# The last batch's routing beside the first half's twenty fixed groups, in one block, in the first expert stage

## The reference

```python
logits = x @ router_w.T + expert_bias[None, :]
probs = sigmoid(logits)
top_w, top_idx = top_k(probs, 8)                   # 8 of 160 experts
top_w = top_w / (sum(top_w) + 1e-09) * 2.5
h1 = silu(einsum('th,eih->eti', x, w_gate))        # 128 -> 64, each expert
routed = einsum('eti,ehi->th', h1 * combine, w_down)
shared = silu(x @ w_gate_shared.T) @ w_down_shared.T
return routed + shared
```

## Time and profile before

| | |
|---|---|
| median of 3 runs | 2836.28 us (2828.25 to 2845.3) |
| profiled execution | 2840.0 us, its span 2838.8 us |
| granted TensorE clock, mean | 0.806 |
| busy: PE / DVE / ACT / POOL | 2002.9 / 1632.1 / 1087.8 / 1264.2 us |
| routing of the last batch | about 862 to 916 us |
| experts, first half / second half | 916 to 1089 us / 1089 to 1275 us |

### The profile page before, as it was taken

One profiled execution on the slowest core, in us unless ns is written; L12 is line 12 of the kernel. 1 busy time (PEld: TensorE's weight loads), 2 busy tenths in 40 slices (PEclk: granted clock), 3 DMA queues, 4 the chain that ended last, 5 costly groups with the idle time before them and its releaser, 6 DMA issues. The chain is left out here.

```text
span 2838.8 us, 45747 instructions
## 1 busy us (share of the span) xinstructions
PE 2002.9 (71%) x15915; PEld 1145.2 (40%) x15915; DVE 1632.1 (57%) x4701; ACT 1087.8 (38%) x2067; POOL 1264.2 (45%) x1244
## 2 busy tenths in 40 slices
PE   5898887877882775665878889888888467676000
PEld 3456455455461554542333333333342255454000
DVE  5457585784777231457776878688783533145222
ACT  0263453453540443440545544443444144444000
POOL 0043166566673444543434420430443444456775
PEclk8899989999995897885787878787887589878555
DMA  9200001000034664554132130121100656555221
GB/s 377 95 1 4 1 6 35 24 12 34 19 131 154 195 209 158 186 177 123 29 90 50 48 82 21 50 74 33 50 29 26 252 182 211 181 187 175 70 59 45
DMA packets 132475, 275.70 MB, mean 97 GB/s; under 512 B 29411, under 2 KB 44387, under 8 KB 127891
## 3 DMA queue, kind: packets, MB, share of 16 engines
q1 hardware_dynamic: 99478, 205.60, 21.8%
q0 software_dynamic: 32768, 67.17, 7.8%
HBM read 146.34 MB, written 125.93 MB: 96 GB/s over the span
## 5 line engine op out<-in xcount | busy, mean ns | idle before, releaser
L1473 POOL DMA_INDIRECT slots_in<-g_xs,g_place x512 | 508.5, 993 | 500.7 <-ACT b_pT L2521 188.6
L2521 ACT ACTIVATE b_pT<-b_psE 128x512 f32<-128x512 f32 (+3 forms) x768 | 330.4, 491 | 469.6 <-PE b_psE L2420 228.9
L2271 DVE TENSOR_REDUCE b_peak<-b_psM 128x1 f32<-128x512 f32 (+3 forms) x768 | 394.5, 551 | 141.5 <-PE b_psM L2403 87.0
L1498 POOL DMA_INDIRECT r_xs<-slots_out,g_place x336 | 333.0, 991 | 312.4 <-ACT b_pT L2521 183.3
L2400 PE MATMUL b_psM<-b_kS,b_qS 72*128 72x512 bf16 (+3 forms) x768 | 283.9, 402 | 66.2 <-DVE b_peak L2271 34.0
L2416 PE MATMUL b_psE<-b_qS,b_kS 75*128 75x512 bf16 (+3 forms) x768 | 258.5, 391 | 57.1 <-ACT b_pT L2521 39.5
L1498 POOL DMA_INDIRECT g_xs<-slots_out,g_place x176 | 172.4, 980 | 124.4 <-issue 48.1
L2060 DVE COPY m_staged_w<-wgd 128x192 f32 x512 | 98.3, 263 | 222.5 <-PE m_psY L2002 114.5
L2060 DVE COPY n_staged_w<-wgd 128x192 f32 x512 | 97.8, 262 | 207.7 <-PE n_psY L2002 147.8
L2430 PE MATMUL b_psV<-b_pT,b_vb 128*32 128x512 f32 (+3 forms) x1536 | 197.3, 597 | 2.5 <-ACT b_pT L2521 2.2
L2400 PEld LDWEIGHTS b_psM<-b_kS,b_qS 72*128 72x128 bf16 x768 | 83.5, 111 | 264.7 <-DVE b_peak L2271 138.6
(11 more groups left out here) (640 smaller groups left out, 4167.3 us busy)
## 6 DMA issues: line engine op xcount, KB each, us to landing
wgd<-in_w_gdT SPq DMA_DIRECT2D x8, 3840.0 KB, 23.0
slots_in<-g_xs SPq DMA_DIRECT2D x26, 1024.0 KB
m_rows<-slots_in SPq DMA_DIRECT2D x104, 256.0 KB
slots_out<-m_y SPq DMA_DIRECT2D x104, 256.0 KB
n_rows<-slots_in SPq DMA_DIRECT2D x104, 256.0 KB
slots_out<-n_y SPq DMA_DIRECT2D x104, 256.0 KB
b_qS<-q_parts SPq DMA_DIRECT2D x48, 192.0 KB
b_kS<-k_parts SPq DMA_DIRECT2D x48, 192.0 KB
```

Source lines behind the costliest of these rows:

```text
L1473: self.nc.gpsimd.indirect_dma_start(self.G.slots_in[self.h], bass.IndirectOffsetOnAxis(self.G.place[:, TPH * self.h + t, k:k + 1], 0), sel ...
L1498: self.nc.gpsimd.indirect_dma_start(self.rows(i)[:, k, :], None, self.G.slots_out[t // TPH], bass.IndirectOffsetOnAxis(self.G.place[:, t, ...
L2271: nc.vector.reduce_max(to, taking()[:, 0:size], AX.X).then_inc(m_taken, 1)
L2521: nc.scalar.activation(pT[:, e % KEPT, h, q0:HALF], psE[:, j % BANKS, q0:HALF], ACT.Exp, scale=SCALE).then_inc(e_taken, 1)
```

## The change

`routed_experts` takes the place of `route` and `experts` for the first stage. In the first half the 20 fixed groups come first, beginning with group 10, whose weights are there already, then the 32 dynamic ones; the second half has the old order. The routing of batch 3 runs beside the fixed groups: TensorE and ScalarE do their parts of it at fixed steps between the groups, VectorE runs all of it before it stages weights. Its SBUF tiles lie in `staged_w`, which no fixed group uses; its PSUM tiles are the second banks of `psY` and `psH`, so the fixed groups have one bank each. The prefix sum over the 160 experts is one scan instruction instead of eight steps. GpSimd sends batch 2's rest with three transfers a group, waits for the places, and sends batch 3's with two a group from the 20th group on. The weights are in ten pieces instead of four, for both stages; five of them are loaded at steps 0, 2, 4, 6 and 8 in the block.

```diff
-CHUNKS = 4
+CHUNKS = 10
...
+def static_first(first):
+    return [((first + i) % STATIC_GROUPS, None) for i in range(STATIC_GROUPS)] + [(STATIC_GROUPS + d, d) for d in range(DYN_GROUPS)]
...
+LOADED_BESIDE_FFN = Beside(STATIC_GROUPS // 2, range(CHUNKS // 2), 0, 2, turn=0, score=1, up=2, down=3, count=8, rank=9, owner=16)
...
+def routed_experts(nc, stage, G, W, S, scatter, last_batch, beside):
...
+        orders = [static_first(beside.first_group), group_order()]
...
+        def h_bank(n):
+            return psH[:, 0 if alone(n) else n % 2, :]
+
+        def y_banks(n):
+            return psY[:, 0 if alone(n) else n % 2, :, :]
...
+                for i in range(HALF_GROUPS):
+                    if i + DEEP < HALF_GROUPS:
+                        sp.wait_ge(x_turned, first + i + 1)
+                        load(first + i + DEEP)
+                    if chunks and i % beside.per == 0:
+                        load_chunk(chunks.pop(0))
+                    store(first + i)
...
+            scatter.upto = TPB * TOPK
+            spaced(scatter, TPB * TOPK - scatter.sent, 0, 3, 1)
+            scatter.of_batch(BATCH - 1)
+            pool.wait_ge(placed, 1)
+            spaced(scatter, TPB * TOPK, STATIC_GROUPS - 1, 2, 1)
...
+            def up(n):
+                g, d = order[n]
+                pe.wait_ge(xT_ready, n + 1)
+                if n and alone(n - 1):
+                    pe.wait_ge(hT_ready, n)
+                elif n >= 2:
+                    pe.wait_ge(hT_ready, n - 1)
...
+            def down(n):
+                g, d = order[n]
+                pe.wait_ge(hT_ready, n + 1)
+                if n and alone(n - 1):
+                    pe.wait_ge(y_ready, n)
+                elif n >= 2:
+                    pe.wait_ge(y_ready, n - 1)
...
+            def last_batch_at(i):
+                if i == beside.turn:
+                    turn_last_batch()
+                if i == beside.score:
+                    score()
+                if i == beside.up:
+                    up_of_shared()
+                if i == beside.down:
+                    down_of_shared()
+                if i == beside.count:
+                    count()
+                if i == beside.rank:
+                    rank()
+                if i == beside.owner:
+                    turn_owner()
...
+                for i in range(HALF_GROUPS):
+                    up(first + i)
+                    if i + 1 < HALF_GROUPS:
+                        turn_rows(first + i + 1)
+                    if i:
+                        down(first + i - 1)
+                    if h == 0:
+                        last_batch_at(i)
...
+                for n in range(first, first + HALF_GROUPS):
+                    squash(n)
+                    if n + 1 < first + HALF_GROUPS:
+                        take_xT(n + 1)
+                    if n > first:
+                        take_y(n - 1)
+                    if h == 0:
+                        last_batch_at(n)
...
+                nc.vector.tensor_tensor_scan(ends, more, more, 0.0, ALU.add, ALU.max)
...
+            norm()
...
+            add_bias()
+            choose()
+            for u in range(2):
+                add_shared(u)
+            plan()
+            find_places()
+            order_weights()
+            write_owners()
+            for c in range(CHUNKS):
+                dve.wait_ge(S.weights_landed[c], 16)
+            for d in range(DYN_GROUPS):
+                stage_weights(0, d)
...
-                route(nc, "m3_", G, W, *part(BATCH - 1), send, expert_loads(G, W, S["m"], range(CHUNKS // 2)))
-                send.of_batch(BATCH - 1)
-                experts(nc, "m", G, S["m"], send)
+                routed_experts(nc, "m", G, W, S["m"], send, part(BATCH - 1), LOADED_BESIDE_FFN)
```

More of the change, by code:

```diff
@@ L2067, in _, with __init__ @@
                 stage_weights(0, d)
+            done = 0
+            for d in range(DYN_GROUPS):
+                stage_weights(1, d)
+                if d % 3 == 2 and d >= 2 * STAGED:
+                    gather.add(dve, done)
+                    done += 1
+            for i in range(done, gather.tiles):
+                gather.add(dve, i)
+class Beside:
+    def __init__(self, first_group, chunks, upfront, per, turn, score, up, down, count, rank, owner):
+        self.first_group, self.chunks, self.upfront, self.per = first_group, list(chunks), upfront, per
+        self.turn, self.score, self.up, self.down, self.count, self.rank, self.owner = turn, score, up, down, count, rank, owner
@@ new lines, with __init__, __call__ @@
+LOADED_BESIDE_FFN = Beside(STATIC_GROUPS // 2, range(CHUNKS // 2), 0, 2, turn=0, score=1, up=2, down=3, count=8, rank=9, owner=16)
+class Carved:
+    def __init__(self, flat):
+        self.flat, self.at = flat, 0
+    def __call__(self, *shape, dtype=F32):
+        n = int(np.prod(shape)) // (2 if dtype == BF16 else 1)
+        ap = self.flat[:, self.at:self.at + n]
+        self.at += n
+        if dtype != F32:
+            ap = ap.bitcast(dtype)
+        return ap if len(shape) == 1 else ap.rearrange("p (t e) -> p t e", e=shape[1])
```

368 lines of the change are left out of this document (added).

## The result

The changed kernel takes 2816.85 us (median of 7 runs, 2811.23 to 2827.45), beside 2836.28 us (median of 7, 2825.67 to 2845.3) for the kernel before: a ratio of 0.9938 [0.9912, 0.9963]. Run again among the first experiments it came to 0.9912 [0.9894, 0.9931].

What follows compares the result with a forecast made beforehand. Routing was taken as a serial VectorE chain, the groups as slowed by each transfer. 25 + 50.8 + 2 + 15 + 109 + 2.5 = 204.3 us against 227.0 gave a 2814 us median, own range 2800 to 2828, overall 2786 to 2840.

Steps and rivals of the forecast that it cites:

- The head: From the stage's first load to the third `m_y`: +25 us, about 8 us of it the price of the routing's company.
- Three a group: Third to fourteenth `m_y`, three transfers beside each group: 4.6 us a group, 50.8 us in all.
- the rank: 24 rank matmuls in one TensorE step beside the fixed groups: estimated 5 us, some 3 slack, so 2 us added.
- Six nearly free groups: Fixed groups 15 to 20, nearly without transfers: 2.5 us each on average, 15 us in all.
- Two a group: Last batch's 64 transfers beside the dynamic groups: 31 groups at 3.51 us, 109 us to the 51st `m_y`.
- What is late next: At the first half's end: the 8.5 us scatter wait goes, and the last group's own `m_y` is late next.
- The slope: In the expert groups: each transfer beside a group lengthens it by 1.08 us, read from two windows.
- A: Beside the groups, transfers cost only issue time: 3.8 us a group with three, 2.96 with two; 2787 us; chance 0.15.
- B: TensorE and VectorE wait for each other in head and steps 8, 9, 16: 12 us more, 2826 us; chance 0.15.
- C: Weight pieces on SyncE's queue are exposed, 23 us, and the gain is gone: 2837 us; chance 0.07.
- D: Transfer runs never break: 6.25 us a group with three, 4.22 with two; 17 us slower, 2853 us; chance 0.08.
- E: VectorE's staging copies hold transfers off in 31 dynamic groups: 50 us above the forecast, 2864 us; chance 0.02.

Runs made afterwards that it cites:

- the second trace: The changed kernel, unaltered, run and traced once more on the same chip as the first experiments: 2817.99 us, 0.9912 of the kernel before.
- runs of five: The kernel before with only its scatter spacing changed, five transfers for three groups instead of three for two: 2903.18 us, ratio 1.0226.
- the memsets: The changed kernel with each of the block's 104 scatter transfers replaced by a GpSimd memset of 128 x 1280, same waits: 2801.42 us.
- the even pairs: Seen in the changed kernel with the second transfer of the last batch's pairs waiting for the next `m_xT`: 2816.48 us, ratio 0.9932.
- the twelve ahead: The changed kernel with ten of batch 2's transfers issued at the block's start, the other thirty two a group: 2814.49 us, ratio 0.9904.
- the forty: The changed kernel with batch 2's 40 transfers issued at once at the block's start instead of three a group: 2849.51 us.

## Why the prediction came out

**The head.** Put at +25, measured at +23.1 (885.68 - 862.62). Without any transfer it is 20.4. The bare head to the third `m_y` is 12 + 2 x 2.26 = 16.5 us, so the routing's company is 4 us and the transfers 2.7, where I had put some 8 down to company alone and nothing to transfers. The size came out, the split did not.

**Three a group.** 4.6 us forecast, 4.66 measured ((936.99 - 885.68) / 11), and the fourteenth at +74.4 instead of +77.8. The size is right and its parts are not. The sum took a group of 1.4 us and 3 x 1.08 for its transfers, and 2 us once for the rank. The runs show 1.96 for the group, 1.16 for the routing's company in each of the eleven, and 1.54 for three transfers as the rest (1.8 by the second trace's 4.90). An overpriced transfer paid for company that I had not priced past the head but for those 2 us. That the two errors came out alike is luck.

**Six nearly free groups.** 15 us forecast, 16.4 measured. The first three take 3.67, 3.47 and 3.38 us with the owners' step among them and the clock at 0.66, the last three 1.96, under the 2.26 of the earlier trace rows, which had been read at the start of a block.

**Two a group.** 109 us forecast from 3.51, 110.1 measured (1063.49 - 953.38), 3.55 a group. The row of the second half was the right neighbour: there gathers came at the same two a group.

**What is late next.** No wait for the scatter, VectorE's chain covered, ten pieces free: as forecast; that ten pieces cost the old order nothing was shown by a run of its own. The sum of 204.3 stands against 203.5.

**The slope.** This is the step that failed, though the sum doesn't show it: "the more transfers a group has beside it, the longer the group: 1.08 us for each". Dynamic groups take 1.96, 2.28 and 3.55 us at none, one and two transfers, and 3.98 at 1.67 in runs of five, where the earlier trace rows had 2.96 at 1.47 in runs of three. Over the free group that is 0.32 us for a transfer that stands alone, 0.68 for one of three ((2.96 - 1.96) / 1.47), 0.80 for one in pairs and fours ((3.55 - 1.96) / 2) and 1.21 for one of five ((3.98 - 1.96) / 1.67). Fives at 1.67 a group are dearer than pairs and fours at 2, so the number alone does not set the price; how they adjoin counts too. No run varied the length of a run at one and the same number and left the rest alone, so how the price is made up of the two stays open. I had read two windows as a line, one all runs of three, the other twenty pairs and twelve fours. It served because the two-a-group part of the changed kernel is like the second window, and because at three a group the routing's unpriced company filled the gap.

**The rivals.** A, issue time only: two transfers issue in 2.5 us and the groups with them take 3.55, where a free one takes 1.96; and the memsets, which keep the same pace, add only 0.15 us to a fixed group. The rule behind it (the Trainium skill, "SBUF — State Buffer", section "SBUF: two separate sides": transfers and compute can't slow each other) does not carry the price of these groups. The instructions keep their lengths (`m_y` 0.60 us in every row), but they start late, 3.80 us in the wait shown. Whatever the path is, the measurement decides. B, company waits: no wait of TensorE on VectorE, but 1.16 us a group are there. C: no wait for rows inside the changed kernel's half, and 1.4 to 2.3 us for each further piece, not 4.6. D was half right, and it is the mechanism behind the sum: runs hold everything, but three a group make runs of six at the longest and not one that never breaks, since GpSimd waits for `m_y` (74.2 us in 30 waits over the block). When the run is forced, the cost it foretold is there. E: no transfer beside copies took over 1.18 us, and most 0.96 to 1.00.

**Where the gain is.** 53.9 us of routing and 8.5 of waiting were taken out, 62.4 together, and 23.5 came back. 38.9 us were given back. The routing's company, measured without transfers, costs the groups 4 us in the head and 11 x 1.16 = 13 behind it. The other 22 were not parted by a run of their own. My reading, not shown, is that they are the transfers, which stand closer than three for two groups, with the 20 among them that the routing had hidden.

**Open.** Why a run of transfers holds ScalarE, VectorE and TensorE is not shown. It isn't GpSimd's being busy (memsets), and it isn't the clock (the even pairs at 1.00). What was held comes back at steps of about 0.7 us from the run's start, as a rule at 7.1 us for five, 5.7 for four, 4.4 for three, 2.0 or 2.8 for two, as if each transfer took two such steps of something that all engines share. The long runs agree: the twelve ahead let a Silu go 17.19 us after their start (880.02 - 862.83), 1.43 each, and the forty the `m_y` after 56.37, 1.41 each. GpSimd starts one each 1.27 us, so by these figures something works a run off more slowly than it is issued; what that is, no run shows. Before, in the routing, the 16 score matmuls stood inside a run of ten of the same transfers (863.91 to 876.29) and took 3.83 us in all. SyncE's stream of small stores and loads, which the groups have and that routing had not, is no sufficient answer: under the run of forty nothing of it moved from 880 to 895 us, and the scores were held all the same. No run here parts the rest.

## What to carry to other kernels

Count not only how many GpSimd transfers stand beside a stage but how they adjoin: one alone cost 0.32 us here, one of a run of five cost four times as much, and a run of forty held the core until it ended. Before a serial stage is laid beside another, look for what already paces that other one, and price the company by a run with that pacer left out, since a slope read from two windows of different arrangement can be right in sum and wrong in its parts. Take a second trace of the same kernel before reading a difference of a few us or a tenth of the clock. When a clock is low in a slow window, test which way the cause runs before pricing by it.

## What the runs showed of the hardware

- An indirect transfer of 128 rows mostly takes GpSimd 0.95 to 1.00 us, 1.26 to 1.31 from start to start in a run. ScalarE's held instruction came back 7.07 to 7.22 us after the start of a run of five (14 of 14), 5.70 to 5.77 after one of four (5 of the 7 in the changed kernel, the other two at 3.53 and 3.59), 2.02 to 2.05 after an even pair. In the kernel before it was 4.32 to 4.42 after one of three (17 of 23); after runs of twelve and forty 17.19 and 56.37. From three on that is 1.41 to 1.47 us a transfer. Under the run of forty TensorE's matmuls started at multiples of 0.70 us from each other.
- At none or one transfer a group the granted clock of the dynamic groups was 1.00, the upper of its two levels (2.4 GHz), at two 0.79 and 0.88 in two traces of the same kernel, with groups of 3.55 and 3.51 us, and 1.00 beside five even pairs in a row, with groups of 3.41; at three, beside the routing, 0.67.
- A GpSimd memset beside float32 copies of VectorE: 89.00 us of VectorE for 207 instructions, against 45.66 for 243 beside transfers.
